# A transformer block on one core: the second batch's projection and routing by 128-token tiles, and ScalarE for the high halves

## The chip, the cores and the metric

One core of one Trainium2 chip runs the whole program. The metric is the device time of one execution in microseconds (us); lower is better. The kernel before took 381.18 us (median of 3 runs, 379.96 to 381.94).

## The reference, cut to what matters

Two batches (b = 0, 1) of 512 tokens with 128 channels go through attention with 16 heads of 8 channels, an output projection, a mixture of eight experts, a scaling by a condition, and a second mixture of experts.

```
x = L0_cond_ref(...)                     # causal attention, then out @ c_proj_w + c_proj_b
scores = einsum('bnd,ed->bne', x, expert_tokens); topk_idx = top_k(scores, 2)
for i in range(8):                       # the first mixture ("FFN0")
    w = mean(topk_idx == i)              # 0, 1/2 or 1 of each token
    y = gelu(gelu(x @ W1[i] + b1) @ W2[i] + b2) @ W3[i] + b3        # 128 -> 512 -> 512 -> 128
    outputs += y * w
x = x + outputs ; L1_cond_ref ; L1_ffn_ref   # scaled weight, then top-2 of 8 experts with a capacity
```

## The kernel before, in words

**Attention.** It goes by groups of four heads: 8 groups, n = 0 to 3 for batch 0 and 4 to 7 for batch 1. A list `schedule` orders three interleaved streams on all engines: score maxima (`score`, `maxT`), scores with exponentials (`s`) and the products with the values (`pv`). For each group the keys go by four chunks of 128 (kc = 0 to 3). ScalarE writes the exponentials into `p_ring` (L872), GpSimd cuts them off above the diagonal (L692), and TensorE adds `p_ring` times `v_sb` into PSUM bank 7 (`values`, L1086 and L1094): four matmuls per chunk, one per head, each in its own 32 columns of the array (`tile_position`). VectorE then copies the bank to `o_sb` (L1559).

**The tail of a batch.** `tail(b)` lists it: four times `on` (L1122, four transposes of 128x128 for a set of 128 tokens with stride 4, L1585 and L1586 for the division by the sum) and `onT` (L1126, L1591), then one projection over 512 tokens `aT` (L1131, L1594), `route` (L1141, L1608 and the choice of two experts), `a` (L1136: back to rows, with the high half L1600, the low half L1601 and a second copy L1605 of the rows in `sent`), `count` and, last, `total`. The tail of batch 0 lies inside group 7's work. That of batch 1 begins when the whole of group 7 is done, and makes the slot numbers (L1625) by which GpSimd scatters rows to the experts' slots in DRAM, 8 indirect DMAs per batch (`dispatch`, L718).

**Weights.** All expert weights are split into two f16 halves. 24 tiles of 512 KB go through a ring of four buffers (`w_ring`): GpSimd issues the load (`load_weights`, L676), ScalarE makes the high half (`high_part`, L847), VectorE the low half (`low_part`, L1506). Tiles 16 to 19 are W3, tiles 20 to 23 the last quarter of W2, which experts 6 and 7 use.

**FFN0.** 23 blocks of 128 rows, one expert each; block i = 0 to 6 is the first block of expert i, and the others come from a table that `block_table` makes. Blocks 0 to 2 are gathered by matmuls with one-hot matrices and do not wait for the scatter; block 3 and later are loaded from the slots (`xg`, L575) and transposed (L1174). The order of an iteration i is written out for each engine:

```
PE   second_layer(i) L1197, first_layer(i+2) L1185, transpose_x(i+3) L1174, transpose_z(i) L1207, third_layer(i-1) L1218
ACT  gelu1(i+2) L883, gelu2(i) L883, high_weights L909, high_part(i+21) L847
DVE  copy_z(i) L1696, copy_x(i+3) L1688/9, split_1(i+2) L1704/6, result(i-1) L1727, split_2(i) L1714/6,
     block_table at i=2, low_part(i+18) for i=3..5, low_weights L1667 for i=6..21
```

A split is two VectorE operations: the high half (a scaled copy to f16) and the low half (scaled value minus high half). `second_layer(6)` waits for all 24 low parts. For i = 6 to 21 the weights of the second mixture are split beside the blocks (`high_weights`, `low_weights`). Iteration 1 has an order of its own, with `gelu2(1)` ahead of `gelu1(3)` and `copy_x(4)` behind `split_2(1)` and `split_1(3)`.

## Time and profile before

| | |
|---|---|
| median of 3 runs | 381.18 us |
| the profiled execution, its own time | 380.43 us |
| its span | 378.7 us |
| busy PE, DVE, ACT, POOL | 295.6, 275.8, 185.2, 155.7 us |
| mean granted TensorE clock | 0.918 of full speed |

The span is what the profiler saw of that one execution; 1.7 us lie around it. Busy times of engines overlap, so they do not add up to the span. What a change is worth is read from the chain of waits at its place.

### The profile page before, as it was taken

The numbers are of one execution on the slowest core, as the hardware profiler recorded it, in microseconds if no ns is written. First come the engines' busy times: TensorE is split into PE (matmuls) and PEld (weight loads), VectorE is DVE, ScalarE is ACT, GpSimd is POOL, SyncE is SP. The second block draws the span as 40 slices with busy tenths as digits, with TensorE's granted clock in tenths as the row PEclk, the third lists the DMA queues.
The fourth block names the chain that finished last, engine by engine and source line by source line (L and its number), as shares of the span: only waits on it lengthen the run. The fifth ranks groups of instructions, "written<-read, shape, count | busy, mean of one in ns | idle before, by whom it ended". The sixth has DMA issues, their size and how long they took to land.

```text
span 378.7 us, 7685 instructions
## 1 busy us (share of the span) xinstructions
PE 295.6 (78%) x2441; PEld 180.4 (48%) x2441; DVE 275.8 (73%) x722; ACT 185.2 (49%) x410; POOL 155.7 (41%) x239
## 2 busy tenths in 40 slices
PE   3957688889897875377976899999987848999910
PEld 2543333333433423164644566666654844687710
DVE  3788769988997564985778488888888689747603
ACT  7650726657675453433624255555553224476602
POOL 8303164645563248763254222332222000577860
PEclk9966989999999999779889899999999988899975
DMA  5589478974530005525247511211000310111114
GB/s 158 200 206 261 162 225 280 246 274 132 159 112 4 1 2 155 184 86 167 78 137 228 145 30 29 64 50 30 23 16 16 111 57 1 34 37 44 50 49 166
DMA packets 21029, 41.75 MB, mean 110 GB/s; under 512 B 3294, under 2 KB 11710, under 8 KB 20992
## 3 DMA queue, kind: packets, MB, share of 16 engines
q0 software_dynamic: 8288, 27.05, 22.7%
q1 hardware_dynamic: 11998, 12.85, 12.5%
q10 hardware_dynamic: 706, 1.38, 1.1%
q8 instruction: 21, 0.34, 0.4%
q14 instruction: 16, 0.13, 0.1%
HBM read 26.59 MB, written 14.43 MB: 108 GB/s over the span
## 4 chain that ended last, share of the span: by engine, by line
PE 33%; DVE 27%; DMA 11%; POOL 11%; issue 10%; ACT 6%; SPq 1%; ACTq 1%; DVEq 0%; POOLq 0%
PE pair L1197 9%; POOL y_rows L790 5%; DVE mA L1569 4%; DMA w_ring<-in_L_ffn_W_dram 3%; PE bank L1094 3%; DVE w_sb L1506 3%; PE bank L1207 3%; PE pair L1185 2%; ACT h L883 2%; PE bank L1218 2%; PE bank L1086 2%; POOL x_slots L718 2%; DVE z L1696 2%; PE pair L1050 2%; POOL tg L779 2%
## 5 line engine op out<-in xcount | busy, mean ns | idle before, releaser
L1197 PE MATMUL pair<-w_sb,h 128*128 (+1 forms) x276 | 66.7, 393 | 3.9 <-DVE w_sb L1506 2.9
L692 POOL TENSOR_SCALAR_AFFINE_SELECT p_ring<-p_ring 128x128 f32<-128x128 f32 (+2 forms) x88 | 38.7, 464 | 58.4 <-ACT p_ring L872 57.8
L872 ACT ACTIVATE p_ring<-bank 128x512 f32<-128x512 f32 (+1 forms) x88 | 44.9, 566 | 32.3 <-PE bank L1073 31.9
L1569 DVE TENSOR_REDUCE mA<-pair 128x2 f32<-128x256 f32 (+3 forms) x64 | 50.4, 817 | 13.2 <-PE pair L1052 13.0
L883 ACT ACTIVATE h<-pair,cols 128x128 f32<-128x128 f32 x92 | 26.2, 368 | 55.9 <-PE pair L1185 54.6
L768 POOL DMA_INDIRECT y_rows<-y_sb,id_now x19 | 23.2, 1223 | 70.6 <-DVE y_sb L1727 66.0
L1197 PEld LDWEIGHTS pair<-w_sb,h 128*128 128x128 f16 x276 | 26.5, 101 | 34.7 <-issue 4.9
L1050 PE MATMUL pair<-kr,qr 128*128 128x128 bf16 (+3 forms) x128 | 34.8, 329 | 6.8 <-DVE mA L1569 5.4
L847 ACT ACTIVATE w_sb<-w_ring 128x1024 f16<-128x1024 f32 x24 | 25.4, 1058 | 29.2 <-DMA w_ring<-in_L_ffn_W_dram 29.2
L883 ACT ACTIVATE h<-bank,cols 128x128 f32<-128x128 f32 x92 | 26.5, 387 | 11.2 <-PE bank L1207 11.1
L1073 PE MATMUL bank<-qr,kr 128*128 128x512 bf16 (+3 forms) x128 | 29.8, 302 | 1.5 <-ACT p_ring L872 1.1
L1506 DVE SCALAR_TENSOR_TENSOR w_sb<-w_ring,w_sb 128x1024 f16<-128x1024 f32 x24 | 29.5, 1228 | 0.1
L1052 PE MATMUL pair<-causal_a,identb 128*128 128x128 bf16 x128 | 27.5, 234 | 0.0
L1050 PEld LDWEIGHTS pair<-kr,qr 128*128 128x128 bf16 x128 | 13.1, 104 | 29.8 <-DVE mA L1569 15.9
L676 POOL DMA_DIRECT2D w_ring<-in_L_ffn_W_dram x24 | 18.4, 772 | 19.0 <-DMA kr<-k_rows 15.7
L779 POOL DMA_INDIRECT tg<-xc_rows,row x10 | 11.2, 1124 | 34.6 <-DVE row L1867 30.1
L1094 PE MATMUL bank<-p_ring,v_sb 128*9 128x512 f32 (+3 forms) x256 | 23.8, 444 | 1.2 <-POOL p_ring L692 1.2
L790 POOL DMA_INDIRECT y_rows<-w_sb,id x20 | 21.2, 1062 | 7.9 <-issue 5.8
L1894 DVE SCALAR_TENSOR_TENSOR hT<-w_sb,hT 128x640 f16<-128x640 f32 x16 | 13.1, 823 | 12.8 <-ACT hT L969 12.8
L1207 PE MATMUL bank<-ident,z 128*128 128x128 f32 x92 | 15.0, 285 | 7.9 <-DVE z L1696 7.0
L1704 DVE TENSOR_SCALAR h<-h 128x512 f16<-128x512 f32 x23 | 9.9, 430 | 14.8 <-ACT h L883 14.8
L1185 PEld LDWEIGHTS pair<-xgT,w_sb 128*128 (+1 forms) x276 | 18.1, 101 | 5.3 <-issue 0.5
(313 smaller groups left out, 606.7 us busy)
## 6 DMA issues: line engine op xcount, KB each, us to landing
w_ring<-in_L_ffn_W_dram POOLq DMA_DIRECT2D x24, 512.0 KB, 5.1
x_slots<-w_sb POOLq DMA_DIRECT2D x4, 1032.0 KB, 8.4
fc_sb<-in_L_ffn_c_fc_dram POOLq DMA_DIRECT2D x4, 512.0 KB, 4.1
cp_sb<-in_L_ffn_c_proj_dram POOLq DMA_DIRECT2D x4, 512.0 KB, 5.6
back<-y_rows SPq DMA_DIRECT2D x8, 256.0 KB, 3.3
kr<-k_rows SPq DMA_DIRECT2D x8, 204.0 KB
qr<-q_rows SPq DMA_DIRECT2D x8, 192.0 KB
xg<-x_slots SPq DMA_DIRECT2D x20, 64.5 KB, 2.1
```

The costliest lines, as they stand in the source:

```text
L692: pool.affine_select(out=probs, in_=probs, compare_op=ALU.is_ge, fill=0.0, base=0, pattern=[[0, heads], [1, P]], channel_multiplier=-1).th ...
L790: pool.indirect_dma_start(y1_d, bass.IndirectOffsetOnAxis(ap=id1[:, j:j + 1], axis=0), z_sb[e // 2][:, c, :], None).then_inc(z_out, 16)
L872: act.activation(p_ring[:, w % P_RING, 0:width], bank(4 + v % 3)[:, 0:width], ACT.Exp).then_inc(exp_done, 1)
L883: ins = act.activation(to[:, c * P:(c + 1) * P], got[:, c * P:(c + 1) * P], ACT.Gelu, bias=cols[:, bass.ds(e * HC + (bias_row + c), 1)], s ...
L1050: mm(to[:, 0:n_keys], qr[:, n % SLOTS, j, t * P:(t + 1) * P], kr[:, n % SLOTS, j, IMG:IMG + n_keys], start=True, stop=False)
L1052: ins = mm(to[:, t * P:n_keys], identb[:, :], causal_a[:, :], start=False, stop=True)
L1073: ins = mm(to[:, i * width:(i + 1) * width], kr[:, n % SLOTS, j0 + i, IMG + kc * P:IMG + (kc + 1) * P], qr[:, n % SLOTS, j0 + i, kc * P:], ...
L1094: ins = mm(bank(7)[32 * j:32 * j + HD + 1, kc * P:], v_sb[:, b, kc, g * G + j, :], p_ring[:, w % P_RING, i * width:(i + 1) * width], start ...
L1197: ins = mm(bank(3), h1[:, s, hq, k * P:(k + 1) * P], w2_sb[k][wq][:, bass.ds(e * HID, HID)], start=(k == 0 and n == 0), stop=(k == HC - 1 ...
L1207: ins = tr(bank(4)[:, m * P:(m + 1) * P], z32[:, m * P:(m + 1) * P], ident[:, :])
L1506: dve.scalar_tensor_tensor(out=lo, in0=w_ring[n % W_RING][:, :], scalar=W_UP, in1=hi, op0=ALU.mult, op1=ALU.subtract).then_inc(w_lo, 1)
L1569: dve.tensor_reduce(mA[:, b, t, g * G + 2 * hp:g * G + 2 * hp + 2], got[:, :, 0:(t + 1) * P], AX_X, ALU.max).then_inc(a_used, 1)
```

## The change

1. **The values of group 7** go into two banks, tokens 0 to 255 into bank 7 and 256 to 511 into bank 3 (`parts_of`). Of chunks 0 and 1 every product becomes two matmuls. Each half is copied to `o_sb` on its own.
2. **The tail of batch 1** leaves `tail(1)` for `last_tail`: tiles of 128 neighbouring tokens, with banks 0, 1, 2 and 7 for the four tiles. The transposes of groups 4 to 6 (`early`) stand behind group 7's chunks 0, 1 and 2; of group 7 one transpose per tile is left. The projection goes in two halves of 256 tokens.
3. **Rows of batch 1**: ScalarE makes the high half from PSUM (`a1_hi`) and the second copy (`a1_copied`); GpSimd waits for the latter before it scatters them.
4. **High halves of the inner activations** (L1704 and L1714) go from VectorE to ScalarE (`hidden_high_1`, `hidden_high_2`), and `result` goes ahead of `split_1`.
5. **Weights**: tiles 16 to 19 are loaded by SyncE's queue as soon as the ring frees each buffer, and ScalarE waits for all four; GpSimd loads tile 21 only when both first `xg` have landed. `low_part` of tiles 17 to 23 stand elsewhere, and the table is made in two halves, at i = 2 and 3.

```diff
-        schedule += tail(1) + [("total",)]
+        ahead = {0: [("early", 0)], 1: [("early", 1)], 2: [("early", 2), ("tile", 0), ("tile", 1)],
+                 3: [("tileT", 0), ("tileT", 1), ("tile", 2), ("tile", 3), ("project", 0, 2), ("tileT", 2),
+                     ("tileT", 3), ("project", 2, 4), ("route1",), ("a1",), ("count1",), ("total1",)]}
...
@@ sync
+            for n in range(W3_FIRST, LAST_PAIR):
+                sp.wait_ge(w_lo, n - W_RING + 1)
+                sp.dma_start(w_ring[n % W_RING][:, :]..., source).then_inc(w3_in, 16)
...
@@ gpsimd
-            for n in range(W3_FIRST, LAST_PAIR):
-                load_weights(n)
...
             load_weights(LAST_PAIR)
+            pool.wait_ge(a1_copied, 1)
             pool.wait_ge(slot_ready, 2)
...
+            for two in range(2):
+                pool.wait_ge(xg_in[two], 16)
             load_weights(LAST_PAIR + 1)
...
@@ scalar
+            act.wait_ge(tail_done, tail_at[("a1",)])
+            act.activation(sent[:, B - 1, 0].bitcast(F16)[:, :, 0:D], bank(0)..., ACT.Copy, scale=IN_UP
+                           ).then_inc(a1_hi, 1)
+            act.wait_ge(tail_used, tail_at[("a1",)])
+            act.copy(sent[:, B - 1, 1].bitcast(F16)[:, :, 0:2 * D], sent[:, B - 1, 0]...).then_inc(a1_copied, 1)
...
+            def hidden_high_1(i):
+                s = i % 2
+                act.wait_ge(gelu1_done, i + 1)
+                if i >= 2:
+                    act.wait_ge(mm2_done, i - 1)
+                act.activation(h1[:, s, 0, :], h32[:, 0], ACT.Copy, scale=IN_UP).then_inc(hi1_ready, 1)
...
@@ tensor
+                elif kind == "tile":
+                    pe.wait_ge(o_ready, groups + first // 2)
+                    tr(bank(TILE_BANKS[first])[:, (NG - 1) * P:], o_sb[:, last_o, tokens], ident[:, :])
+                elif kind == "project":
+                    pe.wait_ge(tail_used, tail_at[("tileT", last - 1)])
+                    mm(bank(4 if first else 6)[:, first * P:last * P], proj_sb[:, :], onT[:, first:last, :]...)
...
@@ vector
-                ts(h1[:, s, 0, :], h32[:, 0], IN_UP, None, ALU.mult).then_inc(hi1_ready, 1)
...
-            low_part(W3_FIRST + 2)
+            low_part(W3_FIRST + 1)
             split_1(0)
             copy_lead(2)
+            low_part(W3_FIRST + 2)
+            split_1(1)
             low_part(W3_FIRST + 3)
-            split_1(1)
...
+                if i:
+                    result(i - 1, of[i - 1])
                 if i + 2 < NB:
                     split_1(i + 2)
-                if i:
-                    result(i - 1, of[i - 1])
                 split_2(i)
-                if i == 2:
-                    block_table()
-                if i >= 3 and i - 2 + LAST_PAIR < W_TILES:
-                    low_part(i - 2 + LAST_PAIR)
+                if i >= 2 and i - 1 + LAST_PAIR < W_TILES:
+                    low_part(i - 1 + LAST_PAIR)
+                if 2 <= i < 4:
+                    block_table(i - 2)
```

TensorE from group 7's first values to the projection, before (L1086 and L1094 are the values, L1073 the scores, L1122 and L1126 the transposes, L1131 the projection):

```order
L1086 MATMUL bank<-pimg,vimg_bd 128x512
L1094 MATMUL bank<-p_ring,v_sb 9x512 x4
L1073 MATMUL bank<-qr,kr 128x256 x4
L1094 MATMUL bank<-p_ring,v_sb 9x384 x4
L1073 MATMUL bank<-qr,kr 128x128 x4
L1094 MATMUL bank<-p_ring,v_sb 9x256 x4
L1094 MATMUL bank<-p_ring,v_sb 9x128 x4
L1122 MATMUL pair<-ident,o_sb 128x128 x8
L1126 MATMUL pair<-ident,on_sb 128x128
L1122 MATMUL pair<-ident,o_sb 128x128 x4
```

And in the change, from behind the values of chunk 1 (L1171 is `early`, six more of which stand behind chunk 0, L1122 the scores, L1155 the values, L1175 `tile`, L1180 `tileT`, L1185 the projection):

```order
L1171 MATMUL pair<-ident,o_sb 128x128 x3
L1122 MATMUL bank<-qr,kr 128x128 x4
L1155 MATMUL pair<-p_ring,v_sb 9x256 x4
L1171 MATMUL bank<-ident,o_sb 128x128 x3
L1175 MATMUL pair<-ident,o_sb 128x128 x2
L1155 MATMUL pair<-p_ring,v_sb 9x128 x4
L1180 MATMUL bank<-ident,on_sb 128x128 x2
L1175 MATMUL pair<-ident,o_sb 128x128
L1175 MATMUL bank<-ident,o_sb 128x128
L1185 MATMUL bank<-onT,proj_sb 128x256
```

Nine transposes now stand ahead of the scores of chunks 2 and 3, and the tail begins before the last values.

ScalarE from the first weight tile of FFN0's loop, before (L883 are the gelus, `bank` those of the second layer; L847 is `high_part`):

```order
L847 ACTIVATE w_sb<-w_ring 128x1024
L883 ACTIVATE h<-bank,cols 128x128 x4
L883 ACTIVATE h<-pair,cols 128x128 x4
L847 ACTIVATE w_sb<-w_ring 128x1024
L883 ACTIVATE h<-pair,cols 128x128 x4
L883 ACTIVATE h<-bank,cols 128x128 x4
```

The same place in the change (L909 are the gelus, L867 `high_part`, L933 and L941 the high halves of the first and the second layer):

```order
L867 ACTIVATE w_sb<-w_ring 128x1024
L909 ACTIVATE h<-bank,cols 128x128 x4
L941 ACTIVATE h<-h 128x512
L909 ACTIVATE h<-pair,cols 128x128 x4
L933 ACTIVATE h<-h 128x512
L867 ACTIVATE w_sb<-w_ring 128x1024
L909 ACTIVATE h<-pair,cols 128x128 x4
L909 ACTIVATE h<-bank,cols 128x128 x4
L933 ACTIVATE h<-h 128x512
L941 ACTIVATE h<-h 128x512
```

From block 2 on, both high halves stand behind both gelus of an iteration.

## Rows read from the trace of the kernel before

**Rows 1.** The page, part 4: shares of the chain that ended last.
```profile
PE 33%; DVE 27%; DMA 11%; POOL 11%; issue 10%; ACT 6%; SPq 1%; ACTq 1%; DVEq 0%; POOLq 0%
```
**Rows 2.** Chain of waits, tail of batch 1 to block 3: start us, us, what.
```profile
143.77 0.64 POOL p_ring L692
...
149.28 0.76 PE pair L1122 x4
...
157.81 0.70 DVE sent L1601
...
160.71 0.98 POOL x_slots L718
...
174.24 4.62 DMA xg<-x_slots
```
**Rows 3.** Timeline, TensorE, group 7's first values and one transposing round: start, us, what.
```profile
139.36 1.10 PE L1086 MATMUL bank<-pimg,vimg_bd 128*128 128x512 f32 x2 [0.92 <-POOL p_ring L692]
...
140.38 1.05 PE L1094 MATMUL bank<-p_ring,v_sb 128*9 128x512 f32 x8
...
141.90 0.83 PE L1094 MATMUL bank<-p_ring,v_sb 128*9 128x384 f32 x8
...
147.85 0.75 PE L1122 MATMUL pair<-ident,o_sb 128*128 128x128 f32 x4 [0.30 <-DVE on_sb L1586]
```
**Rows 4.** Timeline, GpSimd's queue from the last cut to the second scatter.
```profile
144.35 3.54 POOL L676 DMA_DIRECT2D w_ring<-in_L_ffn_W_dram  x4
...
148.19 1.05 POOL L718 DMA_INDIRECT x_slots<-sent,slot  x1 [0.30 <-issue]
...
159.20 0.77 POOL L676 DMA_DIRECT2D w_ring<-in_L_ffn_W_dram  x1
```
**Rows 5.** Timeline, tiles 21 and 22 and block 2's copy.
```profile
172.86 1.51 POOL L676 DMA_DIRECT2D w_ring<-in_L_ffn_W_dram  x2
...
177.22 1.06 ACT L847 ACTIVATE w_sb<-w_ring 128x1024 f16<-128x1024 f32 x1 [2.14 <-DMA w_ring<-in_L_ffn_W_dram]
...
184.94 0.69 DVE L1696 COPY z<-pair 128x512 f32<-128x512 f32 x1
```
**Rows 6.** The page, part 6: DMA issues, count, KB each, us to landing.
```profile
xg<-x_slots SPq DMA_DIRECT2D x20, 64.5 KB, 2.1
```
**Rows 7.** Timeline, block 6.
```profile
207.98 1.22 DVE L1506 SCALAR_TENSOR_TENSOR w_sb<-w_ring,w_sb 128x1024 f16<-128x1024 f32 x1
...
209.26 4.23 PE L1197 MATMUL pair<-w_sb,h 128*128 128x512 f16 x12 [2.89 <-DVE w_sb L1506]
...
213.53 0.69 DVE L1696 COPY z<-pair 128x512 f32<-128x512 f32 x1 [4.33 <-PE pair L1197]
```
**Rows 8.** Timeline, one iteration of the steady loop.
```profile
229.05 0.66 PE L1207 MATMUL bank<-ident,z 128*128 128x128 f32 x4
...
229.97 1.16 ACT L883 ACTIVATE h<-bank,cols 128x128 f32<-128x128 f32 x4
...
230.97 0.68 ACT L909 ACTIVATE cp_sb<-cp_sb 128x512 f16<-128x512 f32 x1
...
231.46 0.42 DVE L1714 TENSOR_SCALAR h<-h 128x512 f16<-128x512 f32 x1
231.91 0.69 DVE L1716 SCALAR_TENSOR_TENSOR h<-h 128x512 f16<-128x512 f32 x1
...
232.52 0.68 DVE L1667 SCALAR_TENSOR_TENSOR cp_sb<-cp_sb 128x512 f16<-128x512 f32 x1
...
233.12 0.68 DVE L1696 COPY z<-pair 128x512 f32<-128x512 f32 x1
...
233.87 0.66 PE L1207 MATMUL bank<-ident,z 128*128 128x128 f32 x4
```
**Rows 9.** Timeline, the last block's copy.
```profile
292.73 0.67 DVE L1696 COPY z<-pair 128x512 f32<-128x512 f32 x1
```
**Rows 10.** Busy us (and instructions) by stretch; then PEclk, DMA share, GB/s.
```profile
274.19:295.40 21.21, 17.45 (x140) 10.53 (x138) 16.13 (x38) 9.65 (x32) 4.98 (x4) 1.00 0.05 15
```

More of the change, by code:

```diff
@@ L413, in build @@
             schedule += merged(first, by_group[n - LAG] if n >= LAG else [])
-        schedule += tail(1) + [("total",)]
-        a_order = [p for p in schedule if p[0] not in ("s", "pv")]
+        ahead = {0: [("early", 0)], 1: [("early", 1)], 2: [("early", 2), ("tile", 0), ("tile", 1)],
+                 3: [("tileT", 0), ("tileT", 1), ("tile", 2), ("tile", 3), ("project", 0, 2), ("tileT", 2),
+                     ("tileT", 3), ("project", 2, 4), ("route1",), ("a1",), ("count1",), ("total1",)]}
+        for kc in range(KC):
+            at_piece = schedule.index(("pv", groups - 1, kc)) + 1
+            schedule[at_piece:at_piece] = ahead[kc]
+        LAST_TAIL = ("early", "tile", "tileT", "project", "route1", "a1", "count1", "total1")
+        tail_at = {p: n + 1 for n, p in enumerate(p for p in schedule if p[0] in LAST_TAIL and p[0] != "early")}
+        a_order = [p for p in schedule if p[0] not in ("s", "pv") + LAST_TAIL]
         a_at = {p: i for i, p in enumerate(a_order)}
@@ L1076, in second_scores, with parts_of @@
                 return ins
+            def parts_of(n, kc):
+                if n < groups - 1:
+                    return [(bank(7), slice(kc * P, S))]
+                return [(bank(LAST_O[h]), slice(max(kc * P, h * S // 2), (h + 1) * S // 2))
+                        for h in range(2) if kc * P < (h + 1) * S // 2]
             def values(n, kc):
@@ L1085, in values @@
                         pe.wait_ge(o_ready, n)
-                    mm(bank(7), vimg_bd[:, b, g * G:(g + 1) * G, :].rearrange("p h c -> p (h c)"),
-                       pimg[:, n % 2, :], start=True, stop=False, skip_group_check=True)
+                    if n == groups - 1:
+                        pe.wait_ge(a_used, len(a_order))
+                    for to, columns in parts_of(n, 0):
+                        mm(to[:, columns], vimg_bd[:, b, g * G:(g + 1) * G, :].rearrange("p h c -> p (h c)"),
+                           pimg[:, n % 2, columns], start=True, stop=False, skip_group_check=True)
                 width = S - kc * P
@@ L1148, in _ @@
                         ins = mm(to[:, 0:E], onesb[:, :], cntb[:, 0, b_, :], start=False, stop=(b_ == b - 1))
-                else:
-                    for b in range(B):
-                        ins = mm(to[:, 0:E], onesb[:, :], cntb[:, 0, b, :], start=(b == 0), stop=(b == B - 1))
                 ins.then_inc(a_done, 1)
@@ L1543, in choose, with counts_of, slots_of @@
                 step(ins)
+            def counts_of(b):
+                choose(b)
+                step(tt(ohsum[:, b], oh[:, 0, b], oh[:, 1, b], ALU.add))
+                step(dve.tensor_reduce(cnt[:, 0, b, :], ohsum[:, b].rearrange("p r e -> p e r"), AX_X, ALU.add))
+                copy(cntb[:, 0, b, :], cnt[:, 0, b, :]).then_inc(cnt_ready, 1)
+            def slots_of(b):
+                for r in range(1, R):
+                    step(tt(rank[:, 0, b, r, :], rank[:, 0, b, r - 1, :], ohsum[:, b, r - 1, :], ALU.add))
+                for k in range(2):
+                    ins = tt(pick[:, k, b], oh[:, k, b], rank[:, 0, b], ALU.mult)
+                step(ins)
+                step(dve.tensor_reduce(slot_f[:, :, b, :], pick[:, :, b], AX_X, ALU.add))
+                copy(slot0[:, :, b, :], slot_f[:, :, b, :]).then_inc(slot_ready, 1)
@@ L1554, in _ @@
                     n, kc = arg
-                    if kc == KC - 1:
+                    if n == groups - 1:
+                        if kc % 2:
+                            half = slice(kc // 2 * 2 * P, kc // 2 * 2 * P + 2 * P)
+                            dve.wait_ge(pv_done, n * KC + kc + 1)
+                            if kc == 1 and n >= O_RING:
+                                dve.wait_ge(a_done, a_at[("on", (n - O_RING) // NG, R - 1)] + 1)
+                            copy(o_sb[:, n % O_RING, half], bank(LAST_O[kc // 2])[:, half]).then_inc(o_ready, 1)
+                    elif kc == KC - 1:
                         dve.wait_ge(pv_done, (n + 1) * KC)
```

166 lines of the change are left out of this document (135 added, 31 removed).

## The prediction

> **What bounds the kernel now.** I read the chain of waits first, then the timelines at the places that the edits touch. No engine bounds the whole: the chain is spread over TensorE, VectorE, transfers and GpSimd [rows 1], so each edit has to be priced at its own place. There are three.
>
> The first is the tail of batch 1. GpSimd's last cut of group 7 ends at 143.77 + 0.64 = 144.41. From there the chain runs through transposes, projection and routing to the slot numbers, and the scatter of batch 1 starts at 160.71. The scatter has landed when SyncE issues the first `xg` at 174.24, and block 3's rows are there 4.62 later, at 178.86 [rows 2]. GpSimd itself is hardly earlier: it issues four loads, then batch 0's scatter from 148.19, and its load of tile 20 ends at 159.20 + 0.77 = 159.97 [rows 4]. So two queues reach the second scatter within a microsecond of each other, and a gain needs both.
>
> The second is the start of FFN0. Tile 21 is issued at 172.86, and ScalarE, which needs it before it goes on to block 1's second gelu, gets it at 177.22 [rows 5]. Later `second_layer(6)` waits 2.89 us for the last low part and then takes 4.23 us [rows 7], where the same 12 matmuls take 2.75 us at the full clock; before it, TensorE had been idle.
>
> The third is the steady loop. One `transpose_z` comes 233.87 - 229.05 = 4.82 after the other, and VectorE goes from a split to a weight's low part to `copy_z` without a gap: 231.91, 232.52, 233.12 [rows 8]. TensorE and VectorE are both nearly full there.
>
> **The change part by part.** The sum is against the profiled execution, 380.43 us (span 378.7 and 1.7 around it); the median of the runs shown is 0.75 above it.
>
> *A, the second scatter: 2.2 earlier.* Ahead of the last cut TensorE gets nine more transposes, 0.75 / 4 = 0.19 each at most [rows 3], less where they overlap: 1.5. The column-split values also stand there. A value product of four heads and 512 columns takes 1.05 (eight records, two passes per head), while a single full-width product takes 1.10 (two records) [rows 3]: the four heads run side by side, and a second pass queued behind a first does not hold up the other heads. Now each head has two calls in a row. At best they cost 0.1 more in all. At worst every pass runs alone: chunk 0 has 16 passes of 256 columns; the x8 row is two passes of 512 one behind the other and some 0.2 of start and end, so 0.43 a pass and 0.21 for 256 columns: 3.4 instead of 1.05, and chunk 1 some 2.6 instead of 0.83, together 4.1 more. I take 0.7, near the low end, since the x8 row is the nearest and shows queued passes that disturb nobody. So the last cut ends 2.2 later, at 146.6. Against that, GpSimd no longer issues the four loads (148.19 - 144.41 = 3.78 until the scatter). Batch 0's scatter with the loads' traffic beside it takes 159.20 - 148.19 = 11.0 [rows 4], without it I say 10.6; with tile 20 and its gap of 0.3 GpSimd is free at 146.6 + 10.6 + 1.1 = 158.3. The loads moved to SyncE's queue cost nothing: it stands idle there, tile 19's buffer is free before group 7's end, and ScalarE would wait only if they landed after 146.
>
> The slot numbers take 16.0 from the last cut before. Two of the four transposing rounds (149.28 - 147.85 = 1.43 each [rows 2, 3]) go, 2.9, and two of the three passes over `sent` (0.6 each, the middle one is the 0.70 of [rows 2]) go to ScalarE, 1.1: 146.6 + 12.0 = 158.6. The copy made by ScalarE starts about 1.5 before the slot numbers are ready and takes about 1.06, as a weight tile's copy of as many elements does [rows 5], so it is hidden; if VectorE's half were late, the scatter would wait for it instead. Scatter 2 starts at about 158.5, 2.2 earlier.
>
> *B, tile 21: 1.7 later.* Its load now waits for both first `xg`. The scatter is done at 174.24 - 2.2 = 172.0, the second `xg` is issued 0.4 after the first and lands after 2.1, the usual time [rows 6], not 4.62 beside two weight loads: 174.5. The tile then lands after 177.22 - 172.86 = 4.36 [rows 5]: 178.9 instead of 177.22. What is queued behind it on ScalarE: `gelu2(1)`, then `gelu1(3)`. On VectorE, `copy_x(4)` stands behind the splits of both, and `first_layer(4)` on TensorE behind that. So block 3's rows come over 4 us earlier, and nearly nothing is won by it.
>
> *C, block 2: 0.5 later in all.* From tile 21 on, the path is 0.9 (its high part), 1.2 (`gelu2(1)`), 0.5 (high half), 1.0 (`gelu1(3)`), 0.7 (high half), 0.6 (low half), 0.3 (`copy_x(4)`), 1.1 (low part of tile 20) and 0.2 more to `copy_z(2)`: 6.5. 178.9 + 6.5 = 185.4, against 184.94 [rows 5].
>
> *D, blocks 2 to 6: 4.1 less.* The low parts are done one iteration earlier, and the table's second half replaces one. `second_layer(6)` loses its wait of 2.89 and runs 4.23 - 2.75 = 1.48 faster [rows 7]: 4.4. At blocks 2 and 3 VectorE still has a low part and half a table ahead of `copy_z`, as much as the whole table before, and the high halves come later: 0.3 back. What is late next there is `copy_z(5)`, by ScalarE's halves.
>
> *E, blocks 6 to 22: 2.8 more.* VectorE loses two operations of about 0.42, and ScalarE gains two of about 0.68 on the same shape [rows 8]. VectorE's work gets shorter but its start gets later, for both high halves stand behind both gelus. The new cycle, from `gelu2` to the next: 1.00 to the high half (229.97 to 230.97), 0.71 until it is seen, 0.61 and 0.61 for the two low halves, 0.60 for the weight's low part, 0.75 from `copy_z` to `transpose_z` (233.12 to 233.87), 0.66 and 0.04 back to ScalarE: 4.98 [rows 8]. With `gelu1` ahead of `gelu2` every second turn I say 5.03, against 4.85 now. Sixteen blocks have a weight's low part: 16 x 0.18 = 2.9, less 0.1 for the end. From `copy_z(6)` to `copy_z(22)` 292.73 - 213.53 = 79.2 [rows 7, 9] becomes 82.0. TensorE's idle share grows to some 8%; the granted clock was still 1.00 in the last stretch, where it is busy for 17.45 of 21.21 [rows 10], so I book no lower clock.
>
> **Sum:** 0.5 - 4.1 + 2.8 = -0.8 (A and B are inside C). 380.43 - 0.8 = 379.6 for such an execution, 380.4 as a median. About 0.5% (1.9 us) is what a measurement of this kernel can tell from no change, so this is "same".
>
> **The rivals.**
>
> *1. The loop loses nothing.* If ScalarE's two copies take 0.5 instead of 0.68, or the high half is seen sooner, the cycle falls to 4.85 or less and TensorE sets the pace again. For it: VectorE has two operations fewer. Against it: the 0.68 is of the very shape and engine [rows 8]. It takes away 2.8: 377.6. It decides from a cycle under 4.9. Chance 0.2.
>
> *2. Tile 21 lands early.* Each microsecond of tile 21 is one of the sum; from a landing before 177.8 on, the whole is faster by over 1.9. With the split products at their best (0.6 earlier) and the tile landing in 3.4 once the scatter has ended (1.0 earlier), it lands at 177.3: 378.8. Chance 0.15. The Trainium skill, "DMA: Bandwidth & Descriptors", section "Anatomy of one DMA", gives about 2.0 us plus the bytes at 436 GB/s, by which 512 KB would take an estimated 3.2; the 4.36 of [rows 5] had other traffic beside it, and by the page the sum would end at 379.2.
>
> *3. Slower: the split heads run one pass at a time.* Then the values cost 4.1 instead of 0.7 more ahead of the last cut, the cut, GpSimd's queue and the slot numbers all slip by 3.4, and tile 21 lands at 182.3: 383.8. The gain of 3.78 in GpSimd's queue is then gone as well. It decides from 3.4 on (0.7 plus the 2.7 between -0.8 and +1.9). Against it: the x8 row. Other ways to this side are a granted clock that falls in the loop's larger gaps. Chance 0.15.
>
> *4. In order, but overlapping by one.* If a head starts with the last pass of the head before, chunk 0 has 13 passes in a row, 2.8, and chunk 1 some 1.9: 2.9 more than before, 2.2 more than I took: 382.6, still within 0.5%. Chance 0.08, within "same". The Trainium skill, "TensorE: Matmul & The Clock Gate", section "The mechanism", says that matmuls start and end strictly in program order; that speaks against this change.
>
> *5. It does not do what it says:* the earlier scatter is worth nothing because tile 21 waits for it. That is in my forecast already, as B.
>
> **How the numbers follow.** My forecast (378.9 to 382) has 0.42, rivals 1 to 4 have 0.2, 0.15, 0.15 and 0.08. Faster 0.35, same 0.42 + 0.08 = 0.5, slower 0.15. The range goes from rival 1 with half of rival 2 (376.6) to rival 3's neighbourhood (383.2), leaving out about 0.1 on either side.
>
> **What would show it.** The last cut of group 7 ends near 146.6 (A; 150 speaks for rival 3); the second scatter starts near 158.5; the first `xg` takes about 2.1 to 2.5 to land; ScalarE gets tile 21 near 178.9 (B); `copy_z(2)` stands near 185.4; `second_layer(6)` takes 2.75 without a wait (D), and `copy_z(6)` comes near 209.9; the loop's period is 5.03 with idle time of VectorE ahead of its low halves, released by ScalarE (E). The prediction is wrong if tile 21 lands over a microsecond off, or if the period is under 4.9 or over 5.15.

## The result, and the profile after

The changed kernel took **387.77 us** (median of 4 runs, 385.38 to 388.69), the kernel before 380.57 beside it: a ratio of 1.0173, 95% interval 1.0124 to 1.0222. It is slower, outside the range of the prediction. The profiled execution took 385.38 (span 383.5), 4.95 more than that of before. It is the fastest of these four; a second profile of the same kernel (c_changed, below) is of an execution of 387.91, at the median. Medians are over all runs and ratios over the fast runs of both kernels alone, so the two can differ.

GpSimd's queue from group 7's last cut to the second half of batch 1's scatter (timeline: start us, us, engine, line, operation, [idle before it, and what ended that]); it answers to [rows 4]:

```profile
144.49 0.64 POOL L708 TENSOR_SCALAR_AFFINE_SELECT p_ring<-p_ring 128x512 f32<-128x512 f32 x1 [0.81 <-ACT p_ring L892]
145.35 1.06 POOL L734 DMA_INDIRECT x_slots<-sent,slot  x1 [0.22 <-issue]
...
156.23 0.77 POOL L692 DMA_DIRECT2D w_ring<-in_L_ffn_W_dram  x1
157.93 0.99 POOL L734 DMA_INDIRECT x_slots<-sent,slot  x1 [0.93 <-DVE slot L1670]
...
165.87 0.95 POOL L734 DMA_INDIRECT x_slots<-sent,slot  x1 [3.16 <-DMA x_slots<-sent,slot]
```

The second scatter starts 2.8 earlier than in [rows 2]. But SyncE's first `xg` goes out at 172.92, only 1.3 earlier: between the fourth and the fifth indirect DMA of this batch GpSimd waits 3.16 until the first twelve of both batches have landed.

Tiles 21 and 22 are issued, and ScalarE gets tile 21 (timeline of GpSimd and of ScalarE, to [rows 5]):

```profile
175.50 1.50 POOL L692 DMA_DIRECT2D w_ring<-in_L_ffn_W_dram  x2 [3.98 <-DMA xg<-x_slots]
...
179.37 1.06 ACT L867 ACTIVATE w_sb<-w_ring 128x1024 f16<-128x1024 f32 x1 [5.29 <-DMA w_ring<-in_L_ffn_W_dram]
```

The chain of waits from block 3's low halves to block 5's second layer (start us, us, what):

```profile
197.84 0.68 DVE h L1881
198.52 1.13 DVE w_sb L1616
199.65 0.11 DVE tabf L1813
...
200.48 0.17 DVE tab L1820
200.67 0.49 SPq L459
...
201.36 3.11 DMA xg<-x_slots
204.47 0.05 issue
204.51 0.40 PE pair L1284 x2
204.91 0.85 PE bank L1317 x4
205.76 1.28 PE bank L1328 x12
207.04 3.15 PE pair L1307 x12
```

This chain has no counterpart before, where the table was done at 191.97 + 0.16 = 192.13 (timeline, VectorE, before):

```profile
191.97 0.16 DVE L1653 TENSOR_SCALAR tab<-tabf 1x16 int32<-1x16 f32 x1
```

Now the table's second half stands behind block 3's splits and a low part (L1616) and is done at 200.64. Only then can SyncE read (L459) where the rows of block 7 lie, the first block that comes from the table; they take 3.11 to land. TensorE waits twice, first for the table itself, which it reads ahead of `first_layer(6)` (L1295) as well, and then for the rows (timeline, TensorE):

```profile
201.33 1.44 PE L1295 MATMUL pair<-xgT,w_sb 128*128 128x128 f16 x12 [2.49 <-DVE tab L1820]
...
204.51 0.40 PE L1284 MATMUL pair<-identh,xg 128*128 128x128 f16 x2 [1.74 <-DMA xg<-x_slots]
```

`transpose_x(7)` (L1284) holds up everything behind it on TensorE: `transpose_z(4)`, `third_layer(3)` and `second_layer(5)`. The last is also slower, 3.36 instead of 2.75 in the first row below. From 201 to 206, with TensorE idle for 2.1 of 5.0 us, the mean granted clock was 0.52, and from 206.8 to 210.2 it was 0.81. Blocks 5 and 6, to [rows 7] (timeline, TensorE):

```profile
206.84 3.36 PE L1307 MATMUL pair<-w_sb,h 128*128 128x512 f16 x12
...
212.22 2.75 PE L1307 MATMUL pair<-w_sb,h 128*128 128x512 f16 x12
```

The wait ahead of `second_layer(6)` is gone, as forecast; another one stands two blocks earlier.

One iteration of the steady loop, to [rows 8] (timeline; TensorE, ScalarE and VectorE in order of time):

```profile
231.42 0.66 PE L1317 MATMUL bank<-ident,z 128*128 128x128 f32 x4 [0.30 <-DVE z L1863]
...
232.22 1.14 ACT L909 ACTIVATE h<-bank,cols 128x128 f32<-128x128 f32 x4
...
233.23 0.64 ACT L933 ACTIVATE h<-h 128x512 f16<-128x512 f32 x1
233.75 0.64 ACT L941 ACTIVATE h<-h 128x512 f16<-128x512 f32 x1
...
234.01 0.69 DVE L1872 SCALAR_TENSOR_TENSOR h<-h 128x512 f16<-128x512 f32 x1 [0.81 <-ACT h L933]
...
234.62 0.68 DVE L1881 SCALAR_TENSOR_TENSOR h<-h 128x512 f16<-128x512 f32 x1
...
235.22 0.68 DVE L1834 SCALAR_TENSOR_TENSOR cp_sb<-cp_sb 128x512 f16<-128x512 f32 x1
...
235.82 0.68 DVE L1863 COPY z<-pair 128x512 f32<-128x512 f32 x1
...
236.56 0.66 PE L1317 MATMUL bank<-ident,z 128*128 128x128 f32 x4 [0.38 <-DVE z L1863]
```

Read it as a ring, a chain that closes on itself and so sets the period, the time from one block to the next. All times are from start to start: `transpose_z` to `gelu2` 0.80, gelu to high half 1.01, until VectorE starts on the low half 0.78, low half, low half, weight's low part 0.61 + 0.60 + 0.60, `copy_z` to `transpose_z` 0.74: 5.14. VectorE now idles 0.81 ahead of its low halves, and TensorE waits for `copy_z`.

**Where the time went.** `copy_z(i)`, once per block, is a good mark to cut the span by. Stretches of the span, us:

| profile | last cut to 2nd scatter | 2nd scatter to first `xg` | copy_z(2) at | copy_z 2 to 6 | copy_z 6 to 22 | copy_z(22) to the end |
|---|---|---|---|---|---|---|
| before | 16.3 | 13.5 | 184.94 | 28.59 | 79.20 | 85.97 |
| changed | 12.8 | 15.0 | 186.12 | 29.22 | 83.56 | 84.60 |
| c_changed | 13.3 | 15.2 | 187.57 | 30.34 | 83.65 | 84.64 |
| e1_table_first | 12.8 | 13.9 | 186.85 | 26.26 | 83.90 | 86.09 |
| e2_halves | 12.8 | 15.8 | 186.62 | 29.44 | 79.12 | 86.02 |
| e3_gate | 12.8 | 15.2 | 184.44 | 30.82 | 83.58 | 85.26 |
| e4_before_halves | 18.9 | 13.2 | 188.03 | 28.80 | 85.05 | 85.72 |
| e5_low_first | 12.8 | 14.3 | 184.87 | 30.09 | 77.90 | 86.34 |
| e6_tail_alone | 13.3 | 15.8 | 185.44 | 29.53 | 79.08 | 85.75 |
| e7_table_and_gate | 12.8 | 15.0 | 184.40 | 26.70 | 83.88 | 86.22 |
| e8_before_low_parts | 19.0 | 13.4 | 189.60 | 24.77 | 78.93 | 86.10 |
| e9_all | 12.8 | 15.0 | 183.78 | 25.59 | 77.82 | 84.61 |
| e10_all_halves_dve | 13.3 | 15.8 | 184.79 | 25.05 | 78.99 | 86.27 |
| e11_no_landing_wait | 12.8 | 11.3 | 182.17 | 25.64 | 77.92 | 86.37 |

From before to changed: 1.18 until `copy_z(2)`, 0.63 from there to `copy_z(6)`, 4.36 in the loop, and 1.37 back in the last stage, together the 4.8 between the spans. The second profile, at the median, splits its 7.5 into 2.6, 1.8 and 4.5, less 1.3: of the loss it has more ahead of `copy_z(6)`, with a granted clock of 0.73 from 144 to 176 where both first profiles had 0.84. The gain in the last stage goes with the clock and not with the change. Here are the second 30 us after `copy_z(22)`, in which the second mixture runs, before and then changed (busy us and instructions of PE, PEld, DVE, ACT, POOL; PEclk, DMA share, GB/s):

```profile
322.73:352.73 30.00, 30.00 (x311) 23.00 (x311) 19.32 (x44) 19.80 (x38) 20.89 (x19) 0.94 0.16 41
```

```profile
328.90:358.90 30.00, 29.98 (x332) 23.56 (x330) 20.05 (x45) 20.99 (x40) 21.89 (x20) 1.00 0.16 43
```

TensorE was busy all through both; the granted clock was 0.94 in one and 1.00 in the other. The three profiles with 84.6 in the last column have 1.00 there, the others 0.94 or 0.95, but for two: e1_table_first and e7_table_and_gate have 1.00 too, and reach the second mixture's gathers 31.4 us after `copy_z(22)` instead of the 29.7 of the changed kernel, which is left open.

### The profile page after: what moved, and what is told of

It reads as the page before. It is cut to its first block, busy times and chain, and to the rows that moved or that the text cites. A ratio compares the mean times of both kernels' runs of the same rounds, so it can differ in the third digit from the quotient of the medians.

```text
span 383.5 us, 7766 instructions
## 1 busy us (share of the span) xinstructions
PE 296.3 (77%) x2461; PEld 185.0 (48%) x2461; DVE 255.7 (67%) x676; ACT 211.6 (55%) x458; POOL 146.7 (38%) x235
## 4 chain that ended last, share of the span: by engine, by line
PE 14%; DVE 12%; POOL 8%; issue 8%; ACT 7%; DMA 5%; ACTq 1%; SPq 1%; POOLq 0%; DVEq 0%
PE pair L1307 6%; ACT h L909 5%; POOL y_rows L807 5%; PE bank L1317 2%; POOL tg L796 2%; DVE z L1863 2%; PE bank L1328 2%; ACT h L933 2%; PE pair L1295 1%; DVE h L1881 1%; DVE h L1872 1%; DMA xg<-x_slots 1%; DMA back<-y_rows 1%; DVE cp_sb L1834 1%; PE bank L1379 1%
## 5 line engine op out<-in xcount | busy, mean ns | idle before, releaser
L1307 PE MATMUL pair<-w_sb,h 128*128 (+1 forms) x276 | 64.8, 385 | 1.3 <-DVE h L1872 1.3
L785 POOL DMA_INDIRECT y_rows<-y_sb,id_now x19 | 18.6, 980 | 79.3 <-DVE y_sb L1892 76.4
L909 ACT ACTIVATE h<-pair,cols 128x128 f32<-128x128 f32 x92 | 26.2, 367 | 38.0 <-PE pair L1295 37.1
L867 ACT ACTIVATE w_sb<-w_ring 128x1024 f16<-128x1024 f32 x24 | 25.1, 1055 | 21.7 <-DMA w_ring<-in_L_ffn_W_dram 20.4
L1122 PE MATMUL bank<-qr,kr 128*128 128x512 bf16 (+3 forms) x128 | 31.6, 316 | 1.4 <-ACT p_ring L892 1.1
L909 ACT ACTIVATE h<-bank,cols 128x128 f32<-128x128 f32 x92 | 26.2, 370 | 10.2 <-PE bank L1317 10.2
L1616 DVE SCALAR_TENSOR_TENSOR w_sb<-w_ring,w_sb 128x1024 f16<-128x1024 f32 x24 | 29.6, 1234 | 0.1
L1872 DVE SCALAR_TENSOR_TENSOR h<-h 128x512 f16<-128x512 f32 x23 | 16.0, 695 | 20.3 <-ACT h L933 20.3
L1295 PE MATMUL pair<-xgT,w_sb 128*128 128x128 f16 x276 | 20.9, 230 | 7.4 <-DVE xgT L1856 4.8
L1099 PEld LDWEIGHTS pair<-kr,qr 128*128 128x128 bf16 x128 | 13.3, 105 | 27.2 <-DVE mA L1748 13.9
L796 POOL DMA_INDIRECT tg<-xc_rows,row x10 | 11.2, 1119 | 35.9 <-DVE row L2033 30.8
L1295 PEld LDWEIGHTS pair<-xgT,w_sb 128*128 (+1 forms) x276 | 18.6, 104 | 12.8 <-DVE xgT L1856 5.6
L1317 PE MATMUL bank<-ident,z 128*128 128x128 f32 x92 | 15.9, 298 | 11.3 <-DVE z L1863 11.2
L692 POOL DMA_DIRECT2D w_ring<-in_L_ffn_W_dram x20 | 14.9, 748 | 23.3 <-DMA kr<-k_rows 15.9
L1155 PE MATMUL bank<-p_ring,v_sb 128*9 128x256 f32 (+3 forms) x240 | 21.4, 428 | 0.5 <-POOL p_ring L708 0.5
```

Of the source, the lines that this page charges most:

```text
L867: act.activation(w_tile(n)[1][0], w_ring[n % W_RING][:, :], ACT.Copy, scale=W_UP).then_inc(w_hi, 1)
L909: ins = act.activation(to[:, c * P:(c + 1) * P], got[:, c * P:(c + 1) * P], ACT.Gelu, bias=cols[:, bass.ds(e * HC + (bias_row + c), 1)], s ...
L1099: mm(to[:, 0:n_keys], qr[:, n % SLOTS, j, t * P:(t + 1) * P], kr[:, n % SLOTS, j, IMG:IMG + n_keys], start=True, stop=False)
L1122: ins = mm(to[:, i * width:(i + 1) * width], kr[:, n % SLOTS, j0 + i, IMG + kc * P:IMG + (kc + 1) * P], qr[:, n % SLOTS, j0 + i, kc * P:], ...
L1295: ins = mm(bank(1 + s)[:, m * P:(m + 1) * P], w1_all[wq][:, bass.ds(e * HID + m * P, P)], xgT[:, s, xq, :], start=(n == 0), stop=(n == len ...
L1307: ins = mm(bank(3), h1[:, s, hq, k * P:(k + 1) * P], w2_sb[k][wq][:, bass.ds(e * HID, HID)], start=(k == 0 and n == 0), stop=(k == HC - 1 ...
```

## The experiments

Three theories stood for the loss: the **late table** (blocks 4 to 6), the **high halves on ScalarE** (the loop), the **wait of tile 21** for `xg`. Each was taken back alone.

**e1_table_first.** The whole table at i = 2, ahead of the low part.

```diff
+                if i == 2:
+                    block_table(0)
+                    block_table(1)
                 if i >= 2 and i - 1 + LAST_PAIR < W_TILES:
                     low_part(i - 1 + LAST_PAIR)
-                if 2 <= i < 4:
-                    block_table(i - 2)
```

> The changed kernel with one edit: at i = 2 the whole table is made, both halves in a row, ahead of the low part of tile 21; the low parts stay at i = 2 to 4. Table theory (the changed kernel makes the table's second half only at 200.6, so the rows of block 7 are asked for at 201.4 and blocks 4 to 6 stretch on the slow clock): the table is ready near 193, the rows of block 7 are asked for by 194, copy_z(5) comes near 205.5 instead of 210.3 and copy_z(6) near 211.5 instead of 215.3; the loop stays at 5.14 per block, the whole is 3 to 4 us faster than the changed kernel, about 384, still slower than the kernel before. Rival (ScalarE's halves, not the table, stretch blocks 4 to 6): copy_z(6) stays within 1 us of 215.3 and the whole within 1 us of the changed kernel's 387.8.

384.12 us (380.44 to 386.09, 12 runs), 1.0044 of before (1.0006 to 1.0081). The end of the table in VectorE's timeline of this run:

```profile
194.46 0.15 DVE L1820 TENSOR_SCALAR tab<-tabf 1x16 int32<-1x16 f32 x1
```

The table was done at 194.6, the rows of block 7 were asked for at once (SyncE at 195.3), no chain ran through them, and `copy_z` 2 to 6 took 26.26 instead of 29.22; `copy_z(6)` came at 213.11, not 211.5, since this execution was 0.7 late at `copy_z(2)` and block 3 carries the whole table. The table theory holds: 3.0 to 4.1 us by the two profiles of the changed kernel, 3.6 by the medians. (Medians of different rounds of runs carry some uncertainty: the kernel before had 380.6 to 381.4.) Over all profiles, the five profiles with the table in halves have 29.2 to 30.8 in that column, the six with an early table and early low parts 24.8 to 26.7.

**e2_halves.** VectorE makes the high halves again, `split_1` ahead of `result`.

```diff
+                ts(h1[:, s, 0, :], h32[:, 0], IN_UP, None, ALU.mult).then_inc(hi1_ready, 1)
...
+                ts(h2[:, s, 0, :], h32[:, 1], IN_UP, None, ALU.mult).then_inc(hi2_ready, 1)
```

> The changed kernel with item 4 undone: VectorE makes both high halves of the inner activations again, with split_1 ahead of result; tail, table, weights and the wait of tile 21 stay as changed. Halves theory (the high halves behind both gelus make the cycle 5.14 instead of 4.87): the period of the steady loop goes back to 4.87, the stretch from copy_z(6) to copy_z(22) from 83.6 to 79.2, the whole is 4 to 5 us faster than the changed kernel: 383. Rival (the longer period comes from the order of the queue, result ahead of the splits, or from the chip): same gain, told apart by the order run. Rival (period is set by TensorE's clock or by the weights' splitting): the period stays above 5.0 and the whole within 1 us of 387.8.

382.56 us (382.02 to 385.42, 12 runs), 1.0055 (1.0021 to 1.0089). The loop took 79.12. The halves theory holds, with the size expected: 4.4 in the stretch, 5.2 by the medians. Blocks 2 to 6 stayed at 29.44, so ScalarE's halves are not what stretches them.

**e3_gate.** The wait of tile 21 taken away.

```diff
-            for two in range(2):
-                pool.wait_ge(xg_in[two], 16)
             load_weights(LAST_PAIR + 1)
```

> The changed kernel with one wait less: GpSimd issues tile 21 as soon as it has sent its eighth indirect DMA and no longer waits for the first two xg. Gate theory: ScalarE gets tile 21 about 2 us earlier, near 177, copy_z(2) comes near 184 instead of 186.1, and the whole is about 2 us faster than the changed kernel, 386. Rival (the two xg land beside the load, as before, and are late themselves): xg takes 4 to 4.6 instead of 2.3, block 3 is late in its place, copy_z(2) and the whole move by less than 0.7.

385.94 us (385.72 to 388.62, 6 runs), 1.0138 (1.0083 to 1.0192). `copy_z(2)` came at 184.44 and `copy_z(4)` at 198.42, 1.7 and 2.1 earlier than in the first profile of the changed kernel, as the theory had it, and then `copy_z(5)` at 210.15 beside 210.32: in this comparison nothing is left. The chain of waits of this run shows where it went:

```profile
198.34 0.17 DVE tab L1818
...
198.53 0.49 SPq L459
...
199.21 4.26 DMA xg<-x_slots
...
206.04 4.07 PE pair L1305 x12
```

The table was 2.1 earlier, but the rows took 4.26 instead of 3.11 to land and the second layer behind them 4.07 instead of 3.15. Neither theory had said that. It isn't shown, though, that the missing wait is the reason: c_changed, which has the wait, took 4.06 for the same rows, and its `copy_z(5)` came at 212.95, later than here. By the medians this run is 1.8 less than the changed kernel, as the theory had it, but the two intervals overlap (1.0083 to 1.0192 and 1.0124 to 1.0222). What the wait costs over the whole with the late table lies between 0 and about 2 us. What it costs at `copy_z(2)` is clearer: over the profiles with the new tail's landing wait, that copy came at 184.87 to 187.57 in the five with the wait of tile 21 and at 183.78 to 185.44 in the five without. And the wait does make the rows land sooner: with it the first `xg` (two or three, median) landed 1.9 to 2.2 after issue in five profiles, without it after 4.0 to 4.5 in nine.

**e4_before_halves.** Item 4 alone, on the kernel before.

> The kernel before with item 4 of the change alone: ScalarE makes both high halves of the inner activations, result goes ahead of split_1. Halves theory: period 5.14 instead of 4.87, copy_z(6) to copy_z(22) 83.6 instead of 79.2, the whole 4 to 5 us slower than the kernel before. Rival (item 4 costs only together with the late table or the new tail): within 1 us of the kernel before.

389.59 us (387.03 to 391.56, 6 runs), 1.0213 (1.0153 to 1.0273): 8 slower, not 4 to 5. Its loop took 85.05, of which 1.1 is in the last block. The other 3 lie ahead of `copy_z(2)`, most of it before the second scatter, where the edit changes nothing. The chain of waits of batch 1's tail in this run, to the 1.11 and 1.04 that the same two steps took before:

```profile
152.51 2.06 PE pair L1154 x2
...
155.49 1.86 PE pair L1164 x8
```

Projection and routing took nearly twice as long (TensorE's granted clock from 144 to 176 was 0.63 on average, and 0.84 before). The profile of the kernel before was of an execution with the full clock here; e8_before_low_parts, with the same tail, had the low one too. So the old tail takes 16.3 or 19 from the last cut to the second scatter. Why this kernel had the low clock is not settled.

**c_changed.** The changed kernel again, beside the next three.

> The changed kernel itself, on the same chip and in the same rounds as the three experiments with it: 386 to 388 us, copy_z periods of 5.13 to 5.14 in the steady loop. Its profile shows how much of a difference between two profiles is no edit's: from copy_z(2) on it should agree with the first one within 0.3 us.

387.68 us (385.06 to 390.99, 6 runs), 1.0155 (1.0100 to 1.0211). The loop agrees within 0.1. `copy_z(2)` came 1.5 later and `copy_z` 2 to 6 was 1.1 longer, against the 0.3 that I had allowed: the rows of block 7 took 4.06 to land instead of 3.11, much as in e3_gate. So a stretch with transfers and a low clock in it repeats within 1 to 1.5 us in these two profiles, the loop within a tenth, and a difference of a microsecond between single profiles ahead of the loop shows nothing.

**e5_low_first.** The halves stay on ScalarE; only the place of the weight's low part changes.

```diff
                 if i:
                     result(i - 1, of[i - 1])
+                if SPLIT_AT < i <= SPLIT_AT + 2 * E:
+                    low_weights(i - 1 - SPLIT_AT)
...
-                if SPLIT_AT <= i < SPLIT_AT + 2 * E:
-                    low_weights(i - SPLIT_AT)
```

> The changed kernel with one move in VectorE's queue: the low part of a second-mixture weight is made one block later, ahead of the splits (low_weights(i - 1) behind result), where VectorE now idles 0.8 us for ScalarE's high half; the copies that ScalarE makes stay. In-order theory (the cycle runs gelu2, high half, two low halves, weight's low part, copy_z, transpose_z, and the 0.60 of the weight's low part is in it only by its place): the cycle falls by up to 0.6, so that TensorE's 4.8 of work per block bounds it; period 4.80 to 4.90, copy_z(6) to copy_z(22) 79 to 80 instead of 83.6, the whole 3.5 to 4.5 us faster than the changed kernel. Rival (ScalarE's time or the wait for its halves sets the period, wherever the weight's low part stands): period stays at 5.1, the whole within 1 us.

382.44 us (380.30 to 384.74, 12 runs), 1.0038 (1.0003 to 1.0073). The period fell to 4.81, shorter than before, and the loop to 77.90. VectorE's timeline in this run:

```profile
231.52 0.29 DVE L1892 SCALAR_TENSOR_TENSOR y_sb<-bank,b_sb 128x128 f32<-128x128 f32 x1
231.73 0.68 DVE L1834 SCALAR_TENSOR_TENSOR fc_sb<-fc_sb 128x512 f16<-128x512 f32 x1
232.89 0.69 DVE L1872 SCALAR_TENSOR_TENSOR h<-h 128x512 f16<-128x512 f32 x1 [0.48 <-ACT h L933]
233.50 0.68 DVE L1881 SCALAR_TENSOR_TENSOR h<-h 128x512 f16<-128x512 f32 x1
234.10 0.68 DVE L1863 COPY z<-pair 128x512 f32<-128x512 f32 x1
```

The weight's low part (L1834) fills the time in which VectorE waits for ScalarE, and `copy_z` stands right behind the second low half. The in-order theory holds: the ring, not the amount of work, set 5.14; it was never the halves alone, but the halves with another 0.60 behind them in one queue.

**e6_tail_alone.** Items 1 to 3 and SyncE's W3 loads alone.

> Items 1, 2, 3 and the first half of 5 alone (values in two banks, tail of batch 1 by tiles, ScalarE's two copies of the rows, W3 loaded by SyncE's queue); high halves on VectorE, the table at i = 2 and the low parts at i = 3 to 5 as in the kernel before, and no wait of tile 21 for xg. Tail theory (the second scatter 2.8 earlier is worth something once tile 21 doesn't wait): copy_z(2) near 183.5 instead of 184.9, copy_z(6) near 212 instead of 213.5, period 4.87, the whole 1 to 2 us faster than the kernel before, 379.5 to 380.5. Rival (it is given back: the transfers of batch 2's scatter and the low part for which second_layer(6) waits come when they came before): copy_z(6) at 213.5 and the whole within 0.7 of the kernel before.

380.76 us (377.98 to 384.34, 12 runs), 0.999 (0.9953 to 1.0027): no difference, so the rival was right about the whole. (`copy_z(6)` at 214.97 was later than either had it.) The second scatter started at 159.28 instead of 160.71, but its first `xg` went out at 175.12, 0.9 later than before, with a landing wait of 3.00 and two indirect DMAs of 1.89 on the way.

**e7_table_and_gate.** The edits of e1_table_first and e3_gate together.

> The changed kernel with both the whole table ahead of the low part at i = 2 and the wait of tile 21 taken away; ScalarE's halves stay. Without that wait alone copy_z(2) and (4) had come 1.7 and 2.1 earlier, but copy_z(5) at the same time, because the rows of block 7 took 4.26 instead of 3.11 to land and the clock was low. Theory that the table hides what the wait costs: now the gain of the wait comes through as well, copy_z(2) near 185, copy_z(5) near 206.5, copy_z(6) near 211.3, the whole 1.5 to 2 us faster than with the table alone (384.1): 382 to 382.6. Rival (the earlier tile 21 is paid for by later xg, table or not): copy_z(6) within 0.5 of 213.1 and the whole at 384.

382.22 us (379.15 to 384.63, 12 runs), 1.0024 (0.9989 to 1.0060). 1.9 less than with the table alone by the medians, though the intervals overlap (1.0006 to 1.0081 there); `copy_z(5)` at 206.41 and `copy_z(6)` at 211.10, where expected, the latter 2.0 ahead of e1_table_first's. With the table early the 2 us of tile 21 come through. That the late table had swallowed them in e3_gate isn't shown: the medians have nearly the same gain there, 1.8.

**e8_before_low_parts.** On the kernel before: low parts of tiles 21 to 23 one iteration earlier, table whole.

```diff
-                if i >= 3 and i - 2 + LAST_PAIR < W_TILES:
-                    low_part(i - 2 + LAST_PAIR)
+                if i >= 2 and i - 1 + LAST_PAIR < W_TILES:
+                    low_part(i - 1 + LAST_PAIR)
```

> The kernel before with one edit: the low parts of tiles 21 to 23 at i = 2 to 4 instead of 3 to 5, at i = 2 behind the whole table. It is the step of the prediction that failed in the change, done without the late table. If that step was right by itself: second_layer(6) loses its wait of 2.89 and its 1.48 of slow clock, copy_z(3) comes 1 later, copy_z(6) at 210 to 210.5 instead of 213.5, the whole 3 to 3.5 us faster than the kernel before: 378. Rival (the wait is only moved: the last tile's high part, at 187.6, or the clock is what is late): copy_z(6) at 213 and the whole within 1 us of 381.2.

378.22 us (374.46 to 381.10, 12 runs) beside 380.94 for the kernel before; but the ratio is 0.9978 (0.9933 to 1.0023), so over the whole the gain isn't established. The stretch shows it: 24.77 instead of 28.59 from `copy_z(2)` to `copy_z(6)`, with a second layer of 2.75 in block 6 and no wait ahead of it. (The profiled execution, of 381.10, is the longest of the twelve; it reached `copy_z(2)` 4.7 later than before.) TensorE's timeline in this run:

```profile
210.91 0.83 PE L1218 MATMUL bank<-w_sb,h 128*128 128x128 f16 x12
211.58 2.75 PE L1197 MATMUL pair<-w_sb,h 128*128 128x512 f16 x12
```

**e9_all.** Changed kernel with the edits of e1, e3 and e5.

> The changed kernel with the three edits together: whole table ahead of the low part at i = 2, no wait of tile 21 for xg, low part of the second mixture's weights one block later and ahead of the splits. High halves on ScalarE. If the causes add: 5.2 from the weights' place and 5.5 from table and wait off 387.7 gives 377; copy_z(6) near 211, period 4.81, copy_z(22) near 289.5. Rival (they overlap: the last stage or the second mixture takes back what the loop gives, since ScalarE and the transfers of its weights are as late): 379 or more.

**374.00 us** (373.23 to 377.14, 6 runs), 0.9888 (0.9819 to 0.9957): faster than both kernels, and 3 less than the sum of the parts. `copy_z(6)` at 209.37 and `copy_z(22)` at 287.19 are 1.6 and 2.3 earlier than expected. Some of this goes with the clock: from 176 to 214 the granted clock was 0.96, in e7_table_and_gate 0.87, and the last stage is 1.6 shorter than there (84.61).

**e10_all_halves_dve.** As e9_all, but with the high halves on VectorE (and so without the moved low part).

> The changed kernel with the whole table ahead of the low part at i = 2, no wait of tile 21, and the high halves back on VectorE (item 4 undone). If the causes add: 387.7 - 5.5 - 4.4 = 377.8, copy_z(6) to copy_z(22) 79.1. It tells with the run before it what ScalarE's halves are worth when their place does no harm: 4.86 against 4.81 per block, 0.8 us; if the halves cost nothing in the blocks 2 to 6 either, the two are within 1 us.

377.55 us (374.96 to 380.41, 12 runs), 0.9947 (0.9902 to 0.9992). 3.5 slower than e9_all, not 0.8. The loop accounts for 1.2 (78.99 against 77.82), and blocks 2 to 6 were 0.5 shorter; the rest is 1.0 until `copy_z(2)` (its first `xg` went out 1.5 later) and 1.7 in the last stage, where the edit changes nothing. ScalarE's halves are worth 1.2 in the loop when nothing stands behind them; the remainder is open.

**e11_no_landing_wait.** e9_all without the wait in the middle of the scatter.

```diff
                 for k in range(2):
-                    if k:
-                        pool.wait_ge(sent0, 16 * 3 * R)
                     dispatch(1, k, slot0, x0_d, sent0)
```

> The same kernel as the run with the three edits together, with GpSimd's wait between the fourth and the fifth indirect DMA of batch 1 (for the landing of the first twelve) taken away. In the kernel before it cost 1.64, in every profile with the new tail 2.96 to 3.45, so that a second scatter which starts 1.4 to 3.0 earlier ends only 0 to 1.3 earlier, or later. If that wait is what eats the tail's gain: the scatter takes 10.5 to 12 instead of 14.0, first xg and tile 21 come 2 to 3 us earlier and the whole is 1.5 to 2.5 us faster than without this edit. Rival (the transfers themselves are late, and waiting for them only moves to SyncE, whose xg waits for all sixteen): first xg within 0.7 and the whole within 0.7.

373.18 us (372.70 to 375.82, 6 runs), 0.9853 (0.9788 to 0.9917). GpSimd's queue, first e9_all, then this run:

```profile
161.84 0.96 POOL L734 DMA_INDIRECT x_slots<-sent,slot  x1 [0.30 <-issue]
165.81 0.96 POOL L734 DMA_INDIRECT x_slots<-sent,slot  x1 [3.01 <-DMA x_slots<-sent,slot]
```

```profile
161.42 0.95 POOL L734 DMA_INDIRECT x_slots<-sent,slot  x1 [0.31 <-issue]
162.68 0.96 POOL L734 DMA_INDIRECT x_slots<-sent,slot  x1 [0.30 <-issue]
```

The scatter took 11.3 instead of 15.0 until the first `xg`, which went out at 168.92 instead of 173.01, and `copy_z(2)` came 1.6 earlier. So the wait was real and not only moved. Of the 4 us, 1.6 reached `copy_z(2)`: in e9_all ScalarE had waited 1.15 for tile 21 and TensorE then 1.02 for block 3's rows; now neither waits, and the path up to there is work of ScalarE, VectorE and TensorE. The medians differ by 0.8, which six runs each (373.23 to 377.14 and 372.70 to 375.82) can't tell from nothing, so over the whole neither expectation is settled. In the profile the last stage (86.37, clock 0.94) is 1.8 longer than e9_all's and takes more than the 1.6 back.

## Why the prediction was wrong

**A, right.** The last cut came at 145.1, not 146.6 (0.4 of that because group 7's values began at 138.96 instead of 139.36): the split value products cost next to nothing. In the timeline of TensorE the sixteen passes of chunk 0 stand as two groups 0.44 apart, from 139.99 to 141.07: 1.08, where the eight full-width ones took 1.05 [rows 3]:

```profile
139.99 0.64 PE L1155 MATMUL bank<-p_ring,v_sb 128*9 128x256 f32 x8
140.43 0.64 PE L1155 MATMUL pair<-p_ring,v_sb 128*9 128x256 f32 x8
141.00 0.88 PE L1171 MATMUL pair<-ident,o_sb 128*128 128x128 f32 x6
```

Rivals 3 and 4, which had 3.4 and 2.8 for these passes, fall with it. So does my use of the Trainium skill, "TensorE: Matmul & The Clock Gate", section "The mechanism", against the change. The same section says that matmuls of different tile positions overlap, although they start and end in order. This trace agrees, with 1.08 for the sixteen passes. The scatter started at 157.9 (158.5 forecast). Not foreseen was that it would then take 15.0 instead of 13.5, so that the first `xg` came only 1.3 earlier, not 2.2.

**B, right in mechanism, 0.5 short.** ScalarE got tile 21 at 179.37 (178.9). The two `xg` took about 2 to land, as taken. The tile took 3.87 from issue to ScalarE, between the 4.36 that I had used [rows 5] and the estimate of 3.2 by the Trainium skill, "DMA: Bandwidth & Descriptors", section "Anatomy of one DMA". The sizes missed each other: `xg` a microsecond later than forecast, the transfer half a microsecond shorter.

**C, right in mechanism, 0.7 short:** `copy_z(2)` at 186.12 instead of 185.4 (187.57 in c_changed, 2.2 short).

**D, the step that failed.** "The low parts are done one iteration earlier, and the table's second half replaces one" counted the table as VectorE's time only. What the table releases was not followed: TensorE's own `first_layer(6)`, SyncE's `xg(7)`, and behind that `transpose_x(7)` on TensorE's in-order queue. It stood in the code (SyncE and TensorE wait for `tab_ready` ahead of block 7), and the table ended 8.5 us later. Instead of 4.1 less, blocks 2 to 6 took 0.6 more. e1_table_first and e7_table_and_gate have 3 to 4 us of it back with this one edit, and e8_before_low_parts shows that the step's own sum was sound: 3.8 instead of 4.1, where the table isn't late. In the five profiles of the changed kernel with an early table the stretch is 1.9 to 3.5 shorter than before; what the rest up to 4.1 is was not separated. "What is late next there is copy_z(5)" was true of the place and wrong of the cause.

**E, right in mechanism, under-sized.** The period is 5.13 to 5.14, not 5.03. The terms that were short: 0.78 instead of 0.71 until the low half starts, and 0.80 instead of 0.70 from `transpose_z` to `gelu2`, since `gelu1` stands ahead of it in every turn and not in every second. ([rows 8] themselves have 0.92 there, 229.05 to 229.97.) And from `copy_z(19)` to `copy_z(22)`, which I had not set apart, 1.2 was lost (16.87 against 15.70): 0.4 per block, against 0.25 in the thirteen before. There VectorE has operations of the last stage as well; the longest of them (L1957) stands in the ring of two blocks, the first of which took 5.80 = 5.14 + 0.66. Together 4.4 instead of 2.8. That this was a cost of the place and not of the engine (e5_low_first) the prediction did not see.

**The sum** by the same terms: 1.2 + 0.6 + 4.4 = 6.2 instead of -0.8. The profiled execution shows 4.95, because its last stage was 1.4 shorter, with the full clock. Of the 7.0 between these two sums, D's failure is 4.7, E's size 1.6, C 0.7. The slower side had a chance of 0.15, for a rival that cost nothing (split heads) and, without a size, for a lower clock in the loop. A late table and a longer end of the loop were in no rival.

## What to carry to other kernels

When an operation is moved in an in-order queue, list what its result releases on every queue, the DMA-issuing ones above all, and price it by the last of these, not by its own duration. Moving work to an idler engine lengthens the ring if the consumer has more work queued behind the hand-over: put independent work into the gap that the hand-over opens (here up to 0.6 per block: with the low part behind the hand-over the loop was 4.4 longer than before, with it in the gap 1.3 shorter). Don't judge a wait of 2 us by one profile of each kernel: two profiles of the changed kernel are 1.5 us apart at `copy_z(2)` and 2.6 at `copy_z(6)`.
